# A mixture of experts: two arrays of sums, three expert steps per dense slot

## The reference, cut to what matters

```python
h = layernorm(x)
xn = w_norm * h * rsqrt(mean(h * h) + EPS)
probs = softmax(xn @ w_router)                 # 32 experts
w_topk, sel = top_k(probs, 4)
...
buf = zeros((E, CAP + 1, H)).at[sorted_e, dest].set(xn[tok])     # at most CAP = 128 tokens per expert
g, u = einsum("ech,ehf->ecf", buf, w_gate), einsum("ech,ehf->ecf", buf, w_up)     # F = 176
y = einsum("ecf,efh->ech", silu(g) * u, w_down)
out = zeros((T, H)).at[tok].add(gath * wv[:, None])              # every token sums its experts' rows
sh = sigmoid(xn @ w_shared_gate) * (silu(xn @ sw_gate) * (xn @ sw_up) @ sw_down)  # shared, F = 704
result = h + out + sh
x = x + 0.5 * result
```

## Time and profile before

| | |
|---|---|
| time, median of 3 runs | 2876.78 us (2868.1 to 2880.69) |
| the profiled execution: its time, its span | 2868.24 us, 2866.5 us |
| TensorE busy | 2626.2 us, 92% of the span |
| VectorE busy | 1950.7 us, 68% |
| ScalarE busy | 1263.9 us, 44% |
| GpSimd busy | 656.0 us, 23% |
| granted TensorE clock, mean | 0.955 |
| DMA | 175.74 MB, 61 GB/s over the span |

### The profile page before, as it was taken

The page is one execution under the profiler, slowest core; times in us unless marked ns, Lnnn a source line. Parts: engine busy times, 40 slices in busy tenths (PEclk is TensorE's granted clock), DMA queues, the critical chain, the costliest instruction groups (busy, mean ns, idle before and its releaser), DMA issues. The chain is left out here.

```text
span 2866.5 us, 39819 instructions
## 1 busy us (share of the span) xinstructions
PE 2626.2 (92%) x14164; PEld 1258.6 (44%) x14164; DVE 1950.7 (68%) x4228; ACT 1263.9 (44%) x1908; POOL 656.0 (23%) x640
## 2 busy tenths in 40 slices
PE   4988999999999999788898997899999999898998
PEld 2442233333333332344555564344445454455665
DVE  6778888887887886487675334867767676486334
ACT  2432466556655667543221221255555556421221
POOL 1454132131231300144001441212111110000442
PEclk8996899999999999999999998799999999999999
DMA  3004331303303210000401663723334430300566
GB/s 121 1 1 104 51 52 21 56 29 46 62 17 51 52 16 1 1 1 1 156 18 42 158 146 90 132 50 54 50 68 62 62 62 2 110 34 17 127 153 174
DMA packets 162592, 175.74 MB, mean 61 GB/s; under 512 B 19090, under 2 KB 135762, under 8 KB 162258
## 3 DMA queue, kind: packets, MB, share of 16 engines
q1 hardware_dynamic: 146948, 152.57, 24.3%
q0 software_dynamic: 12416, 17.84, 3.8%
q10 hardware_dynamic: 3040, 2.88, 0.4%
HBM read 116.32 MB, written 56.13 MB: 60 GB/s over the span
## 5 line engine op out<-in xcount | busy, mean ns | idle before, releaser
L1827 DVE TENSOR_REDUCE a_mx<-a_bank 128x1 f32<-128x512 f32 (+3 forms) x1792 | 1029.1, 627 | 274.2 <-PE a_bank L1564 186.2
L1700 ACT ACTIVATE a_E<-a_bank 128x1024 f32<-128x1024 f32 (+3 forms) x896 | 795.3, 931 | 462.4 <-PE a_bank L1621 317.9
L1564 PE MATMUL a_bank<-a_KT,a_QT 96*128 96x512 bf16 (+4 forms) x1792 | 596.3, 376 | 37.0 <-DVE a_mx L1827 27.4
L1621 PE MATMUL a_bank<-a_QT,a_KT 99*128 99x512 bf16 (+4 forms) x1792 | 508.3, 359 | 4.0 <-DMA a_QT<-a_mT 1.6
L1636 PE MATMUL a_bank<-a_E,a_Vg 128*32 128x512 f32 (+3 forms) x3584 | 438.6, 561 | 0.7 <-ACT a_E L1700 0.7
L1564 PEld LDWEIGHTS a_bank<-a_KT,a_QT 96*128 96x128 bf16 (+1 forms) x1792 | 152.6, 98 | 530.9 <-DVE a_mx L1827 331.1
L1621 PEld LDWEIGHTS a_bank<-a_QT,a_KT 99*128 99x128 bf16 (+1 forms) x1792 | 170.5, 99 | 176.5 <-ACT a_E L1700 35.2
L999 ACT ACTIVATE d_silu<-d_bank 128x512 f32<-128x512 f32 x96 | 57.2, 596 | 361.2 <-PE d_bank L873 357.5
L888 PE MATMUL d_bank<-wdT,d_hT 128*128 128x256 f32 (+1 forms) x768 | 196.9, 400 | 7.5 <-DVE d_hT L1088 7.5
L466 POOL TENSOR_TENSOR f_hl<-f_hT,f_hh 128x512 f16<-128x512 f32 x96 | 111.0, 1156 | 388.4 <-ACT f_hh L485 388.4
L792 POOL DMA_INDIRECT d_xg<-normalised,d_index x64 | 67.5, 1054 | 538.2 <-issue 535.1
(11 more groups left out here) (246 smaller groups left out, 3548.8 us busy)
## 6 DMA issues: line engine op xcount, KB each, us to landing
parts<-a_parts SPq DMA_DIRECT2D x64, 384.0 KB, 2.5
a_QT<-parts SPq DMA_DIRECT2D x180, 128.0 KB, 5.9
a_KT<-parts SPq DMA_DIRECT2D x180, 128.0 KB, 9.2
d_wgu<-in_L_ffn_w_gate SPq DMA_DIRECT2D x64, 176.0 KB
d_wgu<-in_L_ffn_w_up SPq DMA_DIRECT2D x64, 176.0 KB
d_wd<-in_L_ffn_w_down SPq DMA_DIRECT2D x64, 176.0 KB
normalised<-d_xn SPq DMA_DIRECT2D x8, 1152.0 KB, 4.7
acc<-d_zero SPq DMA_DIRECT2D x2, 4224.0 KB, 15.6
```

Of the source, the lines that this page charges most:

```text
L1564: last = nc.tensor.matmul(out[:, 0:w], QT[0:W, h, qt * P:(qt + 1) * P], KT[0:W, h, kh * HALF:kh * HALF + w], start=True, stop=not diag)
L1621: last = nc.tensor.matmul(out, KT[:, h, kt * P:(kt + 1) * P], QT[:, h, half * HALF + c0:(half + 1) * HALF], start=True, stop=not diag)
L1700: nc.scalar.activation(E[:, u % 2, 2 * pair:2 * pair + 2, c0:HALF], bank[:, 2 * pair:2 * pair + 2, c0:HALF], ACT.Exp).then_inc(exps, 1)
L1827: nc.vector.tensor_reduce(mx[:, j, qt, kh:kh + 1], out[:, 0:w], AX.X, ALU.max).then_inc(freed_dve, 1)
```

## The change

The DRAM array `acc` becomes two, `sums`, of the same size: experts with an even number add to the first, those with an odd number to the second. Each add waits only for the one before it to the same array. SyncE zeroes both. `per_slot` takes up to three steps per slot, so that the 35 steps lie in slots 27 to 38. The read-back has sixteen fetches, two for each chunk, through the same four places; `finish(q)` adds both. It runs in slots 41 to 47 for chunks 0 to 6 and in slot 52 for chunk 7.

```diff
-    acc = dram["acc"]
+    acc = dram["sums"]
...
-        k = min(2, NE + LAG - step)
+        k = min(3, NE + LAG - step)
...
-    finishes = {slots[n]: qs for n, qs in ((len(slots) - 7, (0, 1)), (len(slots) - 6, (2,)), (len(slots) - 5, (3,)),
-                                           (len(slots) - 4, (4,)), (len(slots) - 3, (5,)), (len(slots) - 2, (6,)), (len(slots) - 1, (7,)))}
+    finishes = {slots[len(slots) - 12 + q if q < NCH - 1 else len(slots) - 1]: (q,) for q in range(NCH)}
...
-        added = sem(tag + "added", 0)
+        added = [sem(f"{tag}added{a}", 0) for a in range(2)]
...
-                    sp.dma_start(back_in[:, q % ROWS], rows_of(acc, q)).then_inc(back[q % ROWS], 16)
+                    sp.dma_start(back_in[:, q % ROWS], rows_of(acc[q % 2], q // 2)).then_inc(back[q % ROWS], 16)
...
-                sp.dma_start(acc.rearrange("(q p) d -> p q d", p=P), spread(zero[:, 0:D], 1, NT + 1)).then_inc(zeroed, 16)
+                for sums in acc:
+                    sp.dma_start(sums.rearrange("(q p) d -> p q d", p=P), spread(zero[:, 0:D], 1, NT + 1)).then_inc(zeroed, 16)
...
-                sp.wait_ge(added, 16 * NE)
-                for q in range(ROWS):
-                    fetch(q)
+                for a in range(2):
+                    sp.wait_ge(added[a], 16 * NE // 2)
+                for n in range(ROWS):
+                    fetch(n)
                 for q in range(NCH):
                     if final:
-                        sp.wait_ge(finished, START + q + 1)
+                        sp.wait_ge(finished, START + 2 * q + 2)
                         sp.dma_start(rows_of(dram["out"], q), core.x[:, q * CT:(q + 1) * CT, :]).then_inc(sent, 16)
-                    if q + ROWS < NCH:
-                        fetch(q + ROWS)
+                    for n in (2 * q + ROWS, 2 * q + ROWS + 1):
+                        if n < 2 * NCH:
+                            fetch(n)
...
-                    if e:
-                        pool.wait_ge(added, 16 * e)
+                    if e > 1:
+                        pool.wait_ge(added[e % 2], 16 * (e // 2))
...
-                pool.wait_ge(zeroed, START + 16 * 2)
+                pool.wait_ge(zeroed, START + 16 * 3)
...
                         if e > 1:
-                            dve.wait_ge(added, 16 * (e - 1))
+                            dve.wait_ge(added[e % 2], 16 * (e // 2))
...
-                    dve.wait_ge(back[q % ROWS], START + 16 * (q // ROWS + 1))
                     dve.wait_ge(x_done, START + (q + 1) * CT)
-                    nc.vector.tensor_tensor(tiles, tiles, back_in[:, q % ROWS], ALU.add).then_inc(finished, 1)
+                    for n in (2 * q, 2 * q + 1):
+                        dve.wait_ge(back[n % ROWS], START + 16 * (n // ROWS + 1))
+                        if n % 2:
+                            dve.wait_ge(finished, START + n)
+                        nc.vector.tensor_tensor(tiles, tiles, back_in[:, n % ROWS], ALU.add).then_inc(finished, 1)
                     if q < TPB // CT and not final:
-                        dve.wait_ge(finished, START + q + 1)
+                        dve.wait_ge(finished, START + 2 * q + 2)
```

More of the change, by code:

```diff
@@ L797, in add @@
                     pool.wait_ge(y_s, START + e + 1)
-                    if e:
-                        pool.wait_ge(added, 16 * e)
+                    if e > 1:
+                        pool.wait_ge(added[e % 2], 16 * (e // 2))
                     pool.sem_inc(posted, 1)
-                    nc.gpsimd.indirect_dma_start(out=acc, out_offset=bass.IndirectOffsetOnAxis(ap=index[:, e:e + 1], axis=0),
+                    nc.gpsimd.indirect_dma_start(out=acc[e % 2], out_offset=bass.IndirectOffsetOnAxis(ap=index[:, e:e + 1], axis=0),
                                                  in_=ys[:, e % 2, :], in_offset=None, compute_op=ALU.add,
-                                                 bounds_check=NTOK + TRASH - 1, oob_is_err=True).then_inc(added, 16)
-                pool.wait_ge(zeroed, START + 16 * 2)
+                                                 bounds_check=NTOK + TRASH - 1, oob_is_err=True).then_inc(added[e % 2], 16)
+                pool.wait_ge(zeroed, START + 16 * 3)
                 for s in range(2):
@@ L815, in _ @@
                         add(n - LAG)
-                pool.wait_ge(added, 16 * NE)
+                for a in range(2):
+                    pool.wait_ge(added[a], 16 * NE // 2)
             @block.tensor
@@ L1939, in program @@
         dram["xn"] = nc.dram_tensor("normalised", (NTOK + TRASH, D + NE), F32, kind="Internal").ap()
-        dram["acc"] = nc.dram_tensor("acc", (NTOK + TRASH, D), F32, kind="Internal").ap()
+        dram["sums"] = [nc.dram_tensor(f"sums{a}", (NTOK + TRASH, D), F32, kind="Internal").ap() for a in range(2)]
         dram["parts"] = nc.dram_tensor("parts", (B, 2, 3, D, T), BF16, kind="Internal").ap()
```

## The result

The changed kernel takes 2913.2 us (median of 4, 2908.24 to 2916.78), the kernel before, run beside it, 2878.74. The ratio is 1.0128 with a 95% interval of 1.0099 to 1.0157: slower by 1.3%. The forecast was 2914, in a range of 2890 to 2943. The profiled execution of the changed kernel took 2908.24 us with a span of 2906.4; the sum in the prediction gave 2906.0. Runs of one kernel scatter by about half a percent, and the longer ones show the lower mean granted clock (the kernel before, in later runs: 2865.4 us at 0.956, 2888.1 at 0.946).

A forecast was written before the change was run, and what follows sets the result against it. TensorE was taken to bound the kernel. Waits for weights in both expert stages (+40.0 us) and the tails (+1.3, -3.5) gave +37.8, on the median 2876.78 thus 2914.6; predicted 2914, range 2890 to 2943.

The forecast's parts named there:

- What bounds: Expert stage, second mixture: TensorE busy 176.0 of 181.9 us sets the pace; its waits for expert weights are the key.
- Three steps per slot: Expert stage: ten third steps per mixture wait for weights, 23.8 us, plus 0.4 at the start, less 4.2 old idle: +20.0.
- Two arrays: Expert adds: each waits for the add two back, but stalls already space values over 7 us apart against 4.63; no gain or loss.
- The second zeroing: SyncE's queue at a mixture's start: 4224 KB more, first `xn` block up to 15 us late, cost 0, up to 5.
- The read-back: Behind the expert stage: sixteen fetches and adds for eight, hidden under dense slots except 0.6 us in the first mixture.
- The first mixture's gain: First mixture's end: 2.85 us less idle and 2.47 of clock, against 1.25 for an add and 0.6 in two slots: -3.5.
- The second mixture's tail: End of the second mixture: one more add behind the last down projection, +1.25 us.
- the weights are covered after all: Rival for the ten burst slots per mixture: no stall arises, -10 us, 2867 in all; chance 0.04.
- The short stalls: Rival for the expert stage: waits for weights of only 0.95 us each, 5.7 a mixture, 2886 in all; chance 0.08.
- The clock's rival: Rival for the expert stage: TensorE's clock falls in each of 20 stalls, 2 us more each, +78, 2955; chance 0.10.
- the bound behind the stage: Rival from slot 41 on: VectorE's two adds and a late fetch hold TensorE, 3 to 6 us a mixture, 2924; chance 0.08.
- The page on DMA: Skill estimate for an expert's weight load: 4.2 us with issues, 1.7 a stall, 14 us less in total; not used in the sum.

## Why the prediction was right

**What bounds.** TensorE sets the pace of the expert stage and the ring of four places sets where it waits: right, and shown from three sides. More places, an earlier issue and more work between issue and need each take the stalls away; fewer places double their number.

**Three steps per slot.** The forecast was +20.0 us for each mixture: 23.8 us of stalls and 0.4 at the start, less 4.2 of old idle. Measured are +16.2 and +21.6. The stalls are there, each at a third step, and two at a second step in j = 5 slots, which shorten the third step's as the prediction had it. But they sum to 16.7 and 18.5 us and not 23.8. The prediction priced a load at 4.64 us; the sixteen that stand alone (the load before issued about 6 us or more earlier, or none) took 4.0 to 5.4 us from issue to need, 4.2 in the median (the one shown, 2745.71 to 2750.03, took 4.32). The two j = 5 slots wait 2.1 to 2.4 us each and not 3.21. By the windows views TensorE's idle time grew by 13.8 and 15.7 us, its busy time by 2.5 and 6.0. Most of the latter is the clock: one fall in the first mixture's stage, three in the second's, each adding 1.5 to 1.7 us, which the forecast had only as a rival. So the mechanism is right and the sum hit partly by luck: of the forecast 40 us of idle 29.5 came, and 8.5 us of busy time, which the sum had at nothing, filled most of the gap.

**Two arrays.** "Nothing gained, nothing lost" does not hold as it stood, since it was argued from stalls that space the adds. With one array and the same stalls the time is 12 us longer (16 by the ratios), although one add less stands at each end. The term that was mis-sized is the chain of adds: 4.63 us each in the earlier trace rows, over 5 in the middle of the work. It did not enter the sum, because the change brings both edits together.

**The second zeroing.** Cost 0: right. The stretches to slot 27 agree to 0.1 us.

**The read-back.** Under the dense slots it is hidden: the slots 39 to 44 take 30.8 us in the first mixture (1720.80 to 1751.57), in the second 30.7 (2838.16 to 2868.86), and in the second VectorE waits for a fetch only once, 0.6 us. The 0.6 us counted for slots 41 and 42 of the first mixture are 0.1. The second add at each end, +1.25: right, 2.56 us against 1.23. The first mixture's gain, -3.5 forecast, -3.8 measured behind slot 45 (-4.1 forecast there, without the 0.6): right, with 2.52 us of idle left and the matmuls at full clock. The second mixture's tail is 1.9 us above its forecast; 1.7 of it is the clock, which fell behind an idle of 2.52 us, where before 2.33 us had no such effect.

**The rivals.** That the weights are covered after all is refuted by the waits. The short stalls, 0.95 us each, were nearer than a chance of 0.08 says: outside the j = 5 slots the mean is 1.5 us in the first mixture and 1.8 in the second, between them and the 2.17 of the forecast. The clock's rival was right about the mechanism and wrong about how often: four of 24. A fall cost 1.5 to 1.7 us and not 2; with three places, where most stalls last over 4 us, the clock cost 89 us beside 151 us of waits. VectorE did not become the bound behind the stage.

**The page on DMA.** The estimate by the Trainium skill, "DMA: Bandwidth & Descriptors", section "Anatomy of one DMA", was 4.2 us for such a load with its issues. The sixteen loads above took 4.2 us in the median: the page was nearer than the row of 4.64 that the sum used.

## What to carry to other kernels

A ring buffer is deep enough or not by the work that lies between the issue of a load and its use, at the tightest place of the order of work; so when steps are packed more densely, count that distance again for the steps that now stand back to back. First look whether the load can be issued earlier, by freeing each part of a place after its own last reader: here that did what a fifth place does. And read the price of a chain of transfers where other transfers run beside it, not at its quiet end. A deeper buffer in front of such a chain lets the producer run ahead but does not change the chain's pace.

## What the runs showed of the hardware

Idle time of TensorE costs more than itself once the clock falls behind it. In the changed kernel 24 waits for weights lasted 0.6 to 2.4 us, and behind four of them (1.69, 1.71, 2.03 and 2.38 us) the lower level followed. In the three-place kernel it followed behind all 40 stalls of 3.9 to 4.8 us and behind none of the eight of 0.8 to 2.6 us; the mean granted clock of its first stage was 0.80, and 151 us of added waits came with 89 us of added busy time.

Below 3 us the length of the idle alone did not decide: three waits of 1.80 us were followed by no fall, and 2.52 us ahead of the same 48 matmuls gave 12.00 us in one mixture and 13.68 in the other.

A chain of indirect adds to DRAM took 4.5 to 4.7 us an add where no load of weights was issued beside it, and 5.4 us on average (up to 7.0) where one was (the kernel with three buffers for `ys`, second mixture).
